# Second bias of the mixture of experts: added once through the transpose instead of in each gate multiply

## The reference

```python
def _expert_ffn(xf, wa, ba, wb, bb):
    h = xf @ wa.T + ba
    h1, h2 = jnp.split(h, 2, axis=-1)
    h = jax.nn.silu(h1) * h2
    return h @ wb.T + bb
logits = (x @ router_w.T + router_b) / TEMP
topk_val, topk_idx = jax.lax.top_k(logits, K)          # K = 2 of 8 experts
weights = jax.nn.softmax(topk_val, axis=-1)
outs = jax.vmap(_expert_ffn, ...)(xf, w1, b1, w2, b2)  # hidden width 512
combined = (gathered * weights.reshape(-1, K, 1)).sum(axis=1)
...
x = _layernorm(x + _L0_ffn_ref(...), axis=-1)
```

## Time and profile before

| what | value |
| --- | --- |
| median of 3 runs | 2710.08 us (2708.41 to 2713.47) |
| the profiled execution | 2708.41 us |
| its span | 2706.5 us |
| PE busy over the span | 2421.4 us, 89% |
| DVE, ACT, POOL busy | 2029.8, 1435.7, 1052.1 us |
| mean granted PE clock | 0.961 of full |

### The profile page before, as it was taken

The page is one execution under the profiler, slowest core; times in us unless marked ns, Lnnn a source line. Parts: engine busy times, 40 slices in busy tenths (PEclk is TensorE's granted clock), DMA queues, the critical chain, the costliest instruction groups (busy, mean ns, idle before and its releaser), DMA issues.

```text
span 2706.5 us, 40049 instructions
## 1 busy us (share of the span) xinstructions
PE 2421.4 (89%) x14894; PEld 1127.1 (42%) x14894; DVE 2029.8 (75%) x3140; ACT 1435.7 (53%) x2497; POOL 1052.1 (39%) x664
## 2 busy tenths in 40 slices
PE   6799975988868977896789999999999999999897
PEld 4444434453336654665333333333333333333344
DVE  7898876328979956996578888788878887788532
ACT  5576652527547744775335555455545554455462
POOL 1011111207835522553025555455545555455530
PEclk9899988998979999998899999999999999999999
DMA  5000001010000000000100000000000000000000
GB/s 210 0 1 1 1 1 55 1 43 1 31 16 1 1 32 0 2 1 17 43 1 9 9 9 7 7 9 9 9 8 7 9 9 9 10 9 8 6 1 16
DMA packets 21118, 42.04 MB, mean 16 GB/s; under 512 B 10494, under 2 KB 12670, under 8 KB 19644
## 3 DMA queue, kind: packets, MB, share of 16 engines
q1 hardware_dynamic: 20924, 39.48, 4.2%
HBM read 35.03 MB, written 4.45 MB: 15 GB/s over the span
## 4 chain that ended last, share of the span: by engine, by line
PE 60%; DVE 29%; issue 6%; ACT 3%; POOL 0%; DMA 0%; DVEq 0%; POOLq 0%; ACTq 0%; SPq 0%
PE PS L2630 13%; PE PS L2621 12%; PE PS L1227 6%; DVE NR L2834 5%; PE PS L2591 5%; DVE W L2852 2%; DVE NR L274 2%; DVE WK L2179 2%; PE PS L1209 2%; PE PS L671 2%; PE PS L673 2%; PE PS L672 2%; DVE WK L2155 1%; DVE WK L271 1%; PE PS L2577 1%
## 5 line engine op out<-in xcount | busy, mean ns | idle before, releaser
L2834 DVE TENSOR_REDUCE NR<-PS 128x2 f32<-128x1024 f32 x512 | 626.1, 1223 | 208.6 <-PE PS L2592 208.5
L2730 ACT ACTIVATE WK<-PS 128x1024 f32<-128x1024 f32 x512 | 496.7, 1021 | 485.3 <-PE PS L2621 413.1
L2905 POOL TENSOR_TENSOR W<-W,WK 128x1024 f32<-128x1024 f32 x224 | 527.1, 2353 | 477.0 <-DVE W L2852 408.0
L2630 PE MATMUL PS<-WK,W 128*64 128x512 f32 x2048 | 494.1, 603 | 0.0
L2621 PE MATMUL PS<-WK 64*128 64x512 f16 (+1 forms) x4096 | 484.0, 376 | 0.0
L2852 DVE TENSOR_TENSOR W<-W,WK 128x1024 f32<-128x1024 f32 x224 | 284.1, 1268 | 14.4 <-ACT WK L2730 14.3
L2621 PEld LDWEIGHTS PS<-WK 64*128 64x128 f16 (+1 forms) x4096 | 199.0, 94 | 219.2 <-ACT WK L2730 6.5
L2630 PEld LDWEIGHTS PS<-WK,W 128*64 128x64 f32 x2048 | 124.1, 136 | 249.3 <-issue 172.5
L2591 PE MATMUL PS<-WK 64*128 64x512 f16 x512 | 196.2, 383 | 30.3 <-DVE NR L2834 28.6
L2592 PE MATMUL PS<-WK 64*128 64x512 f16 x512 | 196.2, 383 | 0.0
L2194 POOL TENSOR_TENSOR WK<-WK,W 128x512 f32<-128x512 f32 x64 | 113.4, 1792 | 176.6 <-DVE WK L2139 93.8
(11 more groups left out here) (364 smaller groups left out, 4238.9 us busy)
## 6 DMA issues: line engine op xcount, KB each, us to landing
XB<-l_rdens SPq DMA_DIRECT2D x62, 128.0 KB, 2.9
W<-in_mw SPq DMA_DIRECT2D x8, 512.0 KB, 12.4
W<-in_l2w SPq DMA_DIRECT2D x1, 3114.0 KB, 11.9
W<-in_f1w SPq DMA_DIRECT2D x1, 2816.0 KB, 19.1
W<-in_l3w SPq DMA_DIRECT2D x1, 2816.0 KB, 9.4
W<-in_f3w SPq DMA_DIRECT2D x1, 2816.0 KB, 9.6
W<-in_mw SPq DMA_DIRECT2D x8, 256.0 KB, 12.7
la_second_tables<-W SPq DMA_DIRECT2D x1, 2048.0 KB, 6.3
```

Of the source, the lines that this page charges most:

```text
L2630: m = e.matmul(k.PS[64 * i:64 * i + 64, 4, :], self.V[:, kt, g, :], self.PTB[kt // 2 % 2][:, kt % 2, i, :], start=kt == 0, stop=kt == NT - 1)
L2730: e.activation(self.PTB[kt // 2 % 2][:, kt % 2, :, :], self.k.PS[:, 2 * (kt % 2):2 * (kt % 2) + 2, :], ACT.Exp, scale=1.0 / 64).then_inc(s ...
L2834: e.tensor_reduce(self.PM[ji % 2][:, u // 4, :, u % 4], self.k.PS[:, 6:8, :], AX.X, ALU.max).then_inc(self.maxes.sem)
L2905: e.tensor_tensor(ac, ac, p, ALU.add).then_inc(self.acc1.sem)
```

## The change

The second bias leaves the gate multiply. `dve_gate` becomes a plain two-operand multiply, and MB2 with its scaling is gone. The biases are loaded as eight rows of 128 features, padded to 128 rows, so the constants' tile CB grows by 120 columns. For each block G is transposed once more, this time in fp32 and as it is (8 gates by 512 tokens, `pe_gates` with `parts` 0, copied by ACT to GT, which lies in the free part of XT). `pe_rows` turns from four fp32 transposes into four pairs of fp32 matmuls that sum in PSUM: GT with the bias rows, then ACC with the identity.

The two kinds of gate transposes of a block share bank 5 and take turns: for block 0 at jobs 4 (fp32) and 6 (bf16, where it was), for the later blocks at expert 5 (fp32) and expert 6 (bf16, which was at expert 5).

```diff
-        self.MB1, self.MB2 = wk(21504, 64), wk(21568, 8)
+        self.MB1 = wk(21504, 64)
...
+        self.GT = [k.XT[0:8, i * 512:(i + 1) * 512] for i in range(2)]
...
@@ pe
-                if i == 6:
-                    self.pe_gates(e, 0)
+                if i in (4, 6):
+                    self.pe_gates(e, 0, i // 2 - 2)
...
-                elif kb == 0 and x == 5 and b < 3:
-                    self.pe_gates(e, b + 1)
+                elif kb == 0 and x in (5, 6) and b < 3:
+                    self.pe_gates(e, b + 1, x - 5)
...
-    def pe_gates(self, e, b):
+    def pe_gates(self, e, b, parts):
         k = self.k
         if b:
-            e.wait_ge(*self.gs(8 * b - 3))
+            e.wait_ge(*self.gs(8 * b - 3 + parts))
+        elif parts:
+            e.wait_ge(*self.gt(1))
         else:
             e.wait_ge(*self.top(46))
             e.wait_ge(*self.ld.cbb(16))
         for j in range(4):
-            i = e.matmul(k.PS[0:96, 5, j * 128:(j + 1) * 128], self.GP[:, 4 * b + j, :], k.cb("identb"), start=True, stop=True)
+            o = slice(j * 128, (j + 1) * 128)
+            if parts:
+                i = e.matmul(k.PS[0:96, 5, o], self.GP[:, 4 * b + j, :], k.cb("identb"), start=True, stop=True)
+            else:
+                i = e.transpose(k.PS[0:8, 5, o], self.G[:, 4 * b + j, :], k.eye)
         i.then_inc(self.gtr.sem)
...
@@ pe_spread
-            e.wait_ge(*self.gt(1))
-        elif x == 5 and b < 3:
-            e.wait_ge(*self.gt(b + 2))
+            e.wait_ge(*self.gt(2))
+        elif x in (5, 6) and b < 3:
+            e.wait_ge(*self.gt(2 * b + x - 2))
...
@@ pe_rows
         for j in range(4):
-            s_ = slice(j * 128, (j + 1) * 128)
-            i = e.transpose(PS[:, 5, s_], self.ACC[b % 2][:, s_], k.eye)
+            o, s_ = PS[:, 5, j * 128:(j + 1) * 128], slice(j * 128, (j + 1) * 128)
+            e.matmul(o, self.GT[b % 2][:, s_], k.c("mb2", p1=8), start=True, stop=False)
+            i = e.matmul(o, self.ACC[b % 2][:, s_], k.eye, start=False, stop=True)
         i.then_inc(self.otr.sem)
...
@@ act: the same places as in pe
-    def act_gates(self, e, b):
-        e.wait_ge(*self.gtr(b + 1))
-        e.activation(self.G3[0:96, b * 512:(b + 1) * 512], self.k.bank(5, p1=96), ACT.Copy).then_inc(self.gt.sem)
+    def act_gates(self, e, b, parts):
+        k, s_ = self.k, slice(b * 512, (b + 1) * 512)
+        if not parts and b >= 2:
+            e.wait_ge(*self.otr(b - 1))
+        e.wait_ge(*self.gtr(2 * b + parts + 1))
+        if parts:
+            e.activation(self.G3[0:96, s_], k.bank(5, p1=96), ACT.Copy).then_inc(self.gt.sem)
+        else:
+            e.activation(self.GT[b % 2], k.bank(5, p1=8), ACT.Copy).then_inc(self.gt.sem)
...
@@ dve
-        e.tensor_scalar(self.MB2, c("mb2"), 512.0, None, ALU.mult).then_inc(self.bias.sem)
...
@@ dve_gate
-        out = self.TM if x else self.ACC[b % 2]
-        e.scalar_tensor_tensor(out=out, in0=self.k.bank(6 + n % 2), scalar=self.MB2[:, x:x + 1], in1=self.GS[n % 2], op0=ALU.add, op1=ALU.mult).then_inc(self.gated.sem)
+        e.tensor_tensor(self.TM if x else self.ACC[b % 2], self.k.bank(6 + n % 2), self.GS[n % 2], ALU.mult).then_inc(self.gated.sem)
...
-    s["mb2"] = i["L0_ffn_b2"].T
+    s["mb2"] = pad_rows(i["L0_ffn_b2"])
```

More of the change, by code:

```diff
@@ L24 @@
     ("ident", 128), ("bmask", 128), ("hmask", 16), ("sin", 16), ("cos", 16), ("ones", 128),
-    ("b0", 384), ("bo0", 128), ("rb", 8), ("iota8", 8), ("mb1", 64), ("mb2", 8),
+    ("b0", 384), ("bo0", 128), ("rb", 8), ("iota8", 8), ("mb1", 64), ("mb2", 128),
     ("l1bq", 1), ("l1bk", 1), ("l1bkv", 256), ("l1bo", 128), ("decay", 1), ("expn", 128), ("tri", 128),
@@ L610, in __init__ @@
         self.wl = k.counter("moe_w_low", 64)
-        self.bias = k.counter("moe_biases", 2)
+        self.bias = k.counter("moe_biases", 1)
         self.zero = k.counter("moe_gates_zero", 1)
@@ L615, in __init__ @@
         self.gexp = k.counter("moe_gate_exp", 1)
-        self.gtr = k.counter("moe_gates_transposed", 4)
-        self.gt = k.counter("moe_gt", 4)
+        self.gtr = k.counter("moe_gates_transposed", 8)
+        self.gt = k.counter("moe_gt", 8)
         self.up = k.counter("moe_up", 256)
@@ L766, in act @@
                 b, x, kb = self.job(i)
-                if i == 6:
-                    self.act_gates(e, 0)
+                if i in (4, 6):
+                    self.act_gates(e, 0, i // 2 - 2)
                 elif i in (8, 10, 12):
@@ L772, in act @@
                     self.act_spread(e, i // 4)
-                elif kb == 0 and x == 5 and b < 3:
-                    self.act_gates(e, b + 1)
+                elif kb == 0 and x in (5, 6) and b < 3:
+                    self.act_gates(e, b + 1, x - 5)
                 if i >= 4:
@@ L823, in dve @@
         w_low(1, 3)
-        e.wait_ge(*self.bias(2))
+        e.wait_ge(*self.bias(1))
         for i in range(128 + 5):
```

## The result

| | before | changed |
| --- | --- | --- |
| median of 5 runs | 2710.08 us | 2725.35 us |
| lowest to highest | 2708.41 to 2715.16 | 2723.40 to 2728.55 |
| span of the profiled execution | 2706.5 us | 2722.0 us |
| mean granted PE clock | 0.961 | 0.959 |

The ratio is 1.0052 (95% interval 1.0037 to 1.0066): slower by more than the forecast's 7.4 us, 15.3 by the medians, and outside its range. The direction was forecast, the size was not.

What follows compares the result with a forecast made beforehand. PE was taken to set the pace from the second block on, DVE in a stretch of the first. Terms 4.1 + 0.86 - 0.2 + 2.6 = 7.4 us on the 2710.1 median gave 2717.5, range 2711 to 2722.

Steps and rivals of the forecast that it cites:

- (a): Row work of blocks 0 to 2: eight fp32 products at 0.225 us replace four transposes, 1.37 more each, 4.1 us in all.
- The upper bound: Row work: a product at four times a transpose, 0.43 us, giving 3.0 us more per block.
- Dear products: Rival: each row-work product costs 0.43 us, the end twice 3.0 and 0.1 less; 15.6 us, 2726; chance 0.09.
- Cheap products: Rival: the 8-row product hides beside the next one, rows cost 1.4 us, end about 0.9; 3.0 us, 2713; chance 0.13.
- the kind clock: Rival: longer products at the end find or bring back the full clock, also for the next stage; 3.3 us, 2713; chance 0.16.
- (f): Last block's row work at the stage's end, at half clock: 2.7 us more, less 0.1 from gate multiplies, term 2.6.
- (b): New fp32 gate transposes, four per block at 0.43 us: 0.86 us for blocks 2 and 3, hidden for blocks 0 and 1.
- the first block: Two PE halts there leave 1.06 us free, which takes 0.86 of gate transposes; term -0.2 us, up to +0.9 if disturbed.
- (c): Gate multiply with two operands: 32 operations from 745 to 656-691 ns, 1.7 to 2.9 us of DVE time, mostly buying nothing.
- (d): ACT's four more copies, 0.58 us each, covered by ACT's waiting; thin cover at job 4, at most 0.58 us.
- (e): Constants grow by 61 KB, some 0.3 us of transfer, and MB2's scaling goes; both taken as nothing.
- The halts: PE's halt behind the row transposes in each later block, 0.43 us too long, forecast to stay as it is.

Runs made afterwards that it cites:

- e2: Changed kernel with GT padded by zeros to 128 rows, so both products of a pair sum over 128 rows; median 2717.53 us, ratio 1.0035.
- e4: Changed kernel with row work of four fp32 identity products of ACC, none of GT, second bias left out; median 2710.41 us, ratio 1.0001.
- e3: Changed kernel with the earlier row work of four fp32 transposes, second bias left out, gate transposes and copies kept; median 2711.59 us, ratio 1.0007.
- e9: Kernel of PE products alone, no layers, fp32 with 128 columns, various row numbers in turn or alone; 32 and 128 0.42 us, 65 and 128 0.22.
- e1: Changed kernel with only the row work's order changed, four GT products first, then four of ACC; median 2719.49 us, ratio 1.0038; result lacks most of the bias.
- e6: Kernel of PE products alone, no layers, fp32 and bf16, row numbers alone or in turn; fp32 8 and 128 in turn 0.41 us, 128 alone 0.226.
- e7: Changed kernel with the row work of every block done twice, same result; single execution 2755.92 us.
- e8: Kernel with GT padded to 128 rows (e2), with the row work of every block done twice; single execution 2725.67 us.
- e5: Kernel before with only the gate multiply changed to two operands, second bias left out; median 2711.91 us against 2711.89, ratio 1.0003.

## Why the prediction was wrong

**(a), row work of blocks 0 to 2: the step that failed.** The number of products and their place on the path were right; the price of one was not. 0.225 us came from the earlier trace rows, a row of products that all sum over 128 rows. The step said that no row of the 8-row shape was known, and bounded the shape by itself, but the two shapes stand in turn here, and that cost 0.19 us at each of eight changes a block (one at the entry, seven between the products). It made 3.33 us a block with the entry (3.23 and 0.1) against 1.80, three times: 4.6 of the 7.8 us that were missed. The rest is 2.0 at the end and 1.7 of clock, less 0.4 of a halt that fell away. The upper bound, 0.43 a product, held the value, and was set aside for the nearest row.

**Dear products, the rival that had the number.** It gave 15.6 us and 15.3 came, in part by luck: it had 9.0 for the row work and 5.9 for the end where 8.7 and 4.6 were measured, and a fall of the clock that it did not have made up the difference. Its reason was wrong too: it said that weights and products alternate between tiles, and weighed against it that the rows do so too. They do, and e2 alternates as well at 0.224. What differs is the number of rows. The factor of four of the Trainium skill ("TensorE: Matmul & The Clock Gate", glossary entry "xbus") was no reason either: an fp32 product is 0.223 in e4 and a transpose 0.11 in e3, as before. The rule that speaks against this change stands in the Trainium skill, "TensorEngine Tiling (Array Packing)", "Tiling Modes": a change of tiling mode drains the engine, and the modes have 32, 64 or 128 rows. That the number of rows summed over sets the mode of these products is the reading of this text. The runs show the price of a change and not what PE does meanwhile; they agree with the rule, with 0.19 us a change in fp32 and 0.10 in bf16, and the classes of e9. The prediction did not weigh the rule.

**Cheap products and the kind clock, the other rivals.** An 8-row product does not hide beside the next: four of them take 1.08 us in e1, and alone they are 0.22 each in e6. The clock did not hold at the end of the changed kernel, nor in the next stage's first transposes.

**(f), the end.** Forecast 2.6, measured 4.64, nearly all of the excess through the same price: 0.72 us from product to product at half clock against 0.43 in e2, and 5.87 in all against 3.79. The clock was at half there, as taken, and in e2 too, where the step held: 2.56. In e3 and e4 the clock was still at full at this place, so that part of the step was right with some luck.

**The clock behind the row work.** Not forecast: 1.7 us in the profiled execution, less what the halt of block 0 no longer costs. e6 and e9 show falls in products of few rows with PE busy throughout, and e7 against e8 that the doubled row work brings one and the padded one does not. What in few rows brings the clock down stays open.

**(b) and the first block: right.** 0.44 us for four, and the two sets in the first block hidden: the first stretch is 0.20 shorter in e3. The copy at job 4 and the silus queued behind it cost nothing.

**(c): right.** 684 ns, within 656 to 691, and 0.45 us in the stage (e5). **(d), (e): right**, nothing is left for them in e3.

**The halts** behind the row work did not grow. The prediction gave 0.43 us to each later block from the one row it had read, behind block 0's row work; behind block 1's it was 0.26 already before (262.83 to 263.31, less 0.215), and is so in the changed kernel. The one behind block 0's is 0.26 in e2 and e3, and gone in the changed kernel, where PE ran at half clock. Why 0.43 became 0.26 was not explained.

**The range.** 2711 to 2722 left the dear case out at 0.09. The row that the sum went by was near in size and far in surroundings, and the chance was set as if it were near in both.

No version that keeps the second bias beats the kernel before. e2 repairs the changed kernel by 8 us and still pays 7.1 in the stage; what could be gained at most is e5's 0.45.

## What to carry to other kernels

The price of a matmul is that of its sequence: before taking a price from a row, look at what stands before and behind it in the new order, above all at the number of rows summed over. Products of few rows between large ones are best padded with zeros to more than 64 rows; here that took the whole price away (e2). Putting them together in one run cost less too (e1), but that version's result lacked most of the bias, and long runs of 8 or 32 rows lost the clock (e6, e9). And an addend that rides for free in an operation of an engine with slack should not be moved to the engine that sets the pace.

## What the runs showed that was not expected

- A change between 8 or 32 rows, 64 rows, and 65 or more costs 0.19 us with fp32 products of 128 columns, at full clock; between 8 and 128 rows in bf16 it costs 0.10. 96 or 65 beside 128, and 8 beside 32, cost nothing.
- PE can be busy without a pause and lose its clock: in runs of 8 or of 32 rows alone it fell to 1.2 GHz, with 64 rows alone it stayed at 2.4 for 10.8 us.
- Padding with zeros made a product cheaper: 0.224 instead of 0.415 us for sixteen times the rows.
